# One order of the vector work for all inner images, weight taps copied by two engines, and the group mean of x added while x1 is copied

## What is computed

```python
# stage 1, for 8 images b, 64 channels c, on the map padded by one pixel (26 x 26)
g       = group_norm(x)
off     = conv3x3(pad(g), w_off)              # 2 offsets (dy, dx) per channel and pixel
sampled = bilinear(pad(g), grid + off)        # inner 24 x 24 pixels
x1      = x + einsum(relu(batch_norm(sampled) * gamma + beta), w_pw)
# stage 2
cov = covariance(group_norm(x1))              # 64 x 64 for each image
v   = mean_rows(newton_schulz_sqrt(cov, 5 iterations))
a   = sigmoid(w2 @ relu(w1 @ v + b1) + b2)
out = x1 + a * group_norm(x1)
```

## Time and profile before

| | |
|---|---|
| median of 3 runs | 100.12 us (99.66 to 100.27) |
| profiled execution, its own time | 100.33 us |
| its span (first to last instruction) | 98.1 us |
| PE busy / share of the span | 83.1 us (85%) |
| DVE busy | 77.7 us (79%) |
| ACT busy | 63.9 us (65%) |
| chain that ended last, by engine | PE 41%, DVE 35%, ACT 9%, issue 6%, DMA 4% |

### The profile page before, as it was taken

One profiled execution on the slowest core, in us unless ns is written; L12 is line 12 of the kernel. 1 busy time (PEld: TensorE's weight loads), 2 busy tenths in 40 slices (PEclk: granted clock), 3 DMA queues, 4 the chain that ended last, 5 costly groups with the idle time before them and its releaser, 6 DMA issues.

```text
span 98.1 us, 2359 instructions
## 1 busy us (share of the span) xinstructions
PE 83.1 (85%) x873; PEld 58.4 (60%) x873; DVE 77.7 (79%) x262; ACT 63.9 (65%) x141; POOL 17.3 (18%) x41
## 2 busy tenths in 40 slices
PE   5995999999999999999980399999899999898200
PEld 4873655455545554555650289999788888786200
DVE  6659859998699999999999999889945548764420
ACT  2328369995999899877889789249222237784440
POOL 7964997000000000000000482000000000000000
PEclk9999999999999999999998557999999999999555
DMA  2584741989969695693030005000000000000066
GB/s 39 201 260 145 171 136 36 199 262 233 231 176 198 184 189 179 145 246 120 0 120 3 0 0 170 0 0 0 0 7 0 0 3 7 0 0 7 0 246 235
DMA packets 5483, 10.18 MB, mean 104 GB/s; under 512 B 1216, under 2 KB 2272, under 8 KB 5472
## 3 DMA queue, kind: packets, MB, share of 16 engines
q1 hardware_dynamic: 4784, 9.29, 34.6%
q0 software_dynamic: 528, 0.45, 1.8%
q10 hardware_dynamic: 160, 0.30, 1.0%
HBM read 1.92 MB, written 5.14 MB: 72 GB/s over the span
## 4 chain that ended last, share of the span: by engine, by line
PE 41%; DVE 35%; ACT 9%; issue 6%; DMA 4%; ACTq 1%; DVEq 0%
PE ps L702 15%; PE ps L736 7%; DVE rows_at_x L976 6%; PE ps L839 5%; PE ps L780 4%; DMA x_pairs<-in_x_dram 4%; ACT relu_out L610 3%; DVE rows_at_x L991 3%; PE ps L746 3%; DVE rows_at_x L985 3%; DVE row_difference L971 3%; DVE rows_at_x L997 2%; DVE largest_abs_offset L965 2%; DVE neighbour_row L987 2%; DVE rows_at_x L1000 2%
## 5 line engine op out<-in xcount | busy, mean ns | idle before, releaser
L702 PE MATMUL ps<-gmap,w_off_taps 128*64 128x288 f32 (+1 forms) x384 | 38.3, 414 | 1.1 <-DVE w_off_taps L945 1.1
L702 PEld LDWEIGHTS ps<-gmap,w_off_taps 128*64 128x64 f32 (+1 forms) x384 | 19.7, 133 | 18.8 <-issue 6.1
L495 ACT COPY rows_at_x<-x_differences 128x864 f32<-128x864 f32 x8 | 7.3, 916 | 3.2 <-DVE x_differences L953 2.1
L442 POOL DMA_INDIRECT slot_offset<-offset_scratch,gather_rows x1 | 2.1, 2068 | 38.4 <-DVE gather_rows L1056 38.4
L976 DVE COPY_PREDICATED rows_at_x<-positive_offsets,x_differences 128x864 f32<-128x864 int32 x7 | 8.3, 1184 | 0.4 <-ACT positive_offsets L506 0.4
L506 ACT ACTIVATE positive_offsets<-ps 128x576 f32<-128x576 f32 x8 | 5.2, 650 | 4.0 <-PE ps L702 4.0
L488 ACT ACTIVATE gmap<-x_pairs,gn_shift,gn_rstd 64x576 f32<-64x576 f32 x8 | 7.0, 879 | 0.5 <-DVE gn_shift L935 0.4
L736 PEld LDWEIGHTS ps<-ident,x_pairs 128*96 128x96 f32 x48 | 6.7, 198 | 0.4 <-issue 0.4
L736 PE MATMUL ps<-ident,x_pairs 128*96 128x128 f32 x48 | 6.9, 316 | 0.0
L520 ACT ACTIVATE abs_offsets<-offsets 128x576 f32<-128x576 f32 x8 | 6.6, 826 | 0.2
L746 PE MATMUL ps<-w_pw_blocks,relu_out 128*96 128x128 f32 x48 | 6.3, 281 | 0.0
(11 more groups left out here) (209 smaller groups left out, 169.2 us busy)
## 6 DMA issues: line engine op xcount, KB each, us to landing
offset_scratch<-offsets SPq DMA_DIRECT2D x8, 288.0 KB, 3.3
hmap<-gmap SPq DMA_DIRECT2D x16, 98.0 KB, 2.5
gmap_scratch<-gmap SPq DMA_DIRECT2D x8, 196.0 KB, 3.2
gmap<-gmap SPq DMA_DIRECT2D x7, 189.0 KB, 2.8
x_pairs<-in_x_dram SPq DMA_DIRECT2D x4, 288.0 KB, 3.4
out_dram<-result SPq DMA_DIRECT2D x4, 288.0 KB, 2.6
w_off_natural<-in_L_conv_w_off_dram ACTq DMA_DIRECT2D x2, 144.0 KB, 3.8
w_natural<-in_L_conv_w_dram POOLq DMA_DIRECT2D x4, 2.0 KB, 2.4
```

What stands on the lines that cost most here:

```text
L495: nc.scalar.copy(rows3(hrow[:, par]), windows(dx[:, par, 0:HH, 0:W], 3, MC - 1)).then_inc(left_ok, 1)
L702: return mm(ps[out, 2 * par + chunk, 0:Q], wt[rows, slot, out], conv_window(gmap[rows, b], at, NP), start=start, stop=stop)
```

## The change

The images 1 to 6 (`EARLY`) all get image 1's order on DVE: `second_image` becomes `early_image(b, par)` with general indices, and `image_step` is left with images 0, 7 and the closing step. On ACT `left_differences(b)` moves ahead of `positive_parts(b)` for these images. The copy of the first three weight taps is split: ACT copies two (256 columns) ahead of `fill_gmap(0)`, DVE the third (128 columns). `copy_natural` becomes an activation with the mean as its bias, so `x1` holds the mean; the shift becomes `c1 = attention * (rstd * (offset - mean))`, with the factor in parentheses computed by two new small DVE instructions ahead of the pooled vector, and the last four small DVE instructions become three.

```diff
+    EARLY = range(1, 7)
...
             gn1_std(1, 0, 1)
+            act.wait_ge(wtrans, 1)
+            nc.scalar.copy(wt[:, 0:2, :].rearrange("p a n -> p (a n)"), ps[:, 5, 0:2 * P]).then_inc(pairs_ok, 1)
             act.wait_ge(gn1_ok, 1)
...
-                if b == 1:
-                    left_differences(1, 1)
+                if b in EARLY:
+                    left_differences(b, b % 2)
                 positive_parts(b, b % 2)
...
-                    if b > 1:
+                    if b not in EARLY:
                         left_differences(b, b % 2)
                     far_mask(b - 1)
...
-                nc.scalar.copy(x1[:, j], ps[:, NAT_BANK[j % 3], 0:Q]).then_inc(nat_ok, 1)
+                nc.scalar.activation(x1[:, j], ps[:, NAT_BANK[j % 3], 0:Q], ACT.Identity,
+                                     bias=mv1[:, j // 2, 0:1]).then_inc(nat_ok, 1)
...
-                    pe.wait_ge(pairs_ok, 1)
+                    pe.wait_ge(pairs_ok, 2)
...
             dve.wait_ge(wtrans, 1)
-            v.tensor_copy(wt[:, 0:3, :].rearrange("p a n -> p (a n)"), ps[:, 5, 0:3 * P]).then_inc(pairs_ok, 1)
+            dve.wait_ge(pairs_ok, 1)
+            v.tensor_copy(wt[:, 2, :], ps[:, 5, 2 * P:3 * P]).then_inc(pairs_ok, 1)
...
-            def second_image():
+            def early_image(b, par):
+
+                h, g = hrow[:, par], hrow[:, 1 - par]
+                dve.wait_ge(along, 4 * b)
                 v.tensor_tensor(vd[:], g[:, 0], g[:, 1], ALU.subtract).then_inc(across, 1)
+                dve.wait_ge(across, 2 * b - 1)
+                v.tensor_tensor(vd[:], vd[:], ab[:, 1 - par, 0], ALU.mult).then_inc(across, 1)
+                dve.wait_ge(across, 2 * b)
+                v.tensor_tensor(xd[:, b - 1], vd[:], g[:, 1], ALU.add).then_inc(image_done, 1)
+                dve.wait_ge(left_ok, b + 1)
+                dve.wait_ge(pos_ok, b + 1)
...
+                differences(b + 1, 1 - par)
...
-            second_image()
-            for b in range(2, B - 1):
-                image_step(b, b % 2)
+            for b in range(1, B - 1):
+                if b in EARLY:
+                    early_image(b, b % 2)
+                else:
+                    image_step(b, b % 2)
             image_step(B - 1, 1, ahead=False, between=locate_slot)
...
+            v.tensor_tensor(rstd_offset[:], vals[:, 1], mv1[:, :, 0], ALU.subtract).then_inc(rstd_offset_ok, 1)
+            dve.wait_ge(rstd_offset_ok, 1)
+            v.tensor_tensor(rstd_offset[:], rstd_offset[:], vals[:, 0], ALU.mult).then_inc(rstd_offset_ok, 1)
             dve.wait_ge(vec_ps, 1)
...
             dve.wait_ge(att_ok, 1)
-            link(v.tensor_tensor(ar[:], att[:], vals[:, 0], ALU.mult))
-            then(v.tensor_tensor(c1[:], ar[:], vals[:, 1], ALU.mult))
-            v.tensor_scalar(s1[:], ar[:], 1.0, None, ALU.add)
+            dve.wait_ge(rstd_offset_ok, 2)
+            then(v.tensor_tensor(ar[:], att[:], vals[:, 0], ALU.mult))
+            then(v.tensor_tensor(c1[:], att[:], rstd_offset[:], ALU.mult))
             wait()
-            v.tensor_tensor(c1[:], c1[:], mv1[:, :, 0], ALU.add).then_inc(out_scale_ok, 1)
+            v.tensor_scalar(s1[:], ar[:], 1.0, None, ALU.add).then_inc(out_scale_ok, 1)
             dve.wait_ge(out_scale_ok, 1)
```

More of the change, by code:

```diff
@@ L109, in deform_conv_then_covariance_attention @@
         count = sb("far_count", [P, 1])
+        rstd_offset = sb("rstd_times_offset", [P, T])
         most = sb("far_images_and_places_beyond_two", [1, 1])
@@ L290, in deform_conv_then_covariance_attention @@
         att_ps = sem("attention_in_psum")
+        rstd_offset_ok = sem("rstd_times_offset_ready")
         out_scale_ok = sem("out_scale_ready")
@@ new lines, in early_image @@
+                dve.wait_ge(across, 2 * b - 1)
[4 more added lines that the diff above has]
+                dve.wait_ge(pos_ok, b + 1)
+                v.copy_predicated(rows3(h), windows(rows(pos[:, par, 1, :]), 3, 0).bitcast(i32),
+                                  windows(dx[:, par, 0:HH, 1:1 + W], 3, MC - 1)).then_inc(along, 1)
@@ new lines, in early_image @@
+                differences(b + 1, 1 - par)
+                dve.wait_ge(along, 4 * b + 1)
+                v.copy_predicated(h[:, 0], pos[:, par, 0, :].bitcast(i32), h[:, 2]).then_inc(chosen, 1)
+                dve.wait_ge(above_ok, b + 1)
+                v.copy_predicated(rows(mrow[:, par]), rows(pos[:, par, 0, :]).bitcast(i32),
+                                  hmap[:, b, 2:2 + HH, 1:1 + W]).then_inc(chosen, 1)
+                dve.wait_ge(chosen, 2 * b + 1)
+                dve.wait_ge(off_ok, b + 1)
@@ L1030, in second_image @@
+                v.tensor_tensor(h[:, 0:2], h[:, 0:2], windows(off[:, b, :, 1], 2, 0), ALU.mult).then_inc(along, 1)
+                dve.wait_ge(abs_ok, b + 1)
+                v.tensor_tensor(far[:, b], ab[:, par, 0], ab[:, par, 1], ALU.max).then_inc(far_ok, 1)
+                dve.wait_ge(along, 4 * b + 2)
+                v.tensor_tensor(rows(h[:, 1]), rows(h[:, 1]), hmap[:, b, 1:1 + HH, 1:1 + W],
                                 ALU.add).then_inc(along, 1)
-                dve.wait_ge(chosen, 4)
@@ L1032, in second_image @@
-                v.tensor_tensor(h[:, 0], h[:, 0], mrow[:, 1], ALU.add).then_inc(along, 1)
+                dve.wait_ge(chosen, 2 * b + 2)
+                v.tensor_tensor(h[:, 0], h[:, 0], mrow[:, par], ALU.add).then_inc(along, 1)
             def zero_far(g, b0, b1):
```

23 lines of the change are left out of this document (removed).

## The result

| | before | changed |
|---|---|---|
| median of 20 runs each, same chips | 100.25 us (99.30 to 101.38) | 100.69 us (100.02 to 101.62) |
| ratio of the times, 95% interval | | 1.0062 [1.0032, 1.0092] |
| profiled execution, its own time | 100.33 us | 101.32 us |
| its span | 98.1 us | 99.1 us |
| mean granted TensorE clock, share of full | 0.927 | 0.945 |

The change makes the kernel 0.6% slower, within the 1% called "no change" ahead of it. The forecast was 100.6 us. A ratio leaves out executions over 1.5% above the fastest of their kernel: one of the 20 of the changed kernel, and further down three of 12 of the kernel with only image 7's list new, four of 12 where that kernel has no pairs. Executions of one kernel also differ by their mean granted clock.

A forecast was written before the change was run, and what follows sets the result against it. DVE's own throughput from 25.3 to 54.3 us was taken to set the end. +0.52 (image 7, start included) + 0.09 (bias) - 0.12 (end) = +0.49 on 100.12 gave 100.6 us; own range 100.2 to 101.1, 8 in 10 99.7 to 101.5.

The forecast's parts named there:

- What bounds it: DVE's own throughput from 25.3 to 54.3 us sets the end; counts and transposes hang on the release by `gather_rows`.
- The wait goes, three stalls come: DVE, images 2 to 6: the 1.12 us wait goes; three stalls of 0.12 make an image 5.47 instead of 5.12.
- The first rival, no stalls: Dependent pairs on DVE cost nothing, images stay 5.12 us: -0.82 with the edges, 99.3 us; chance 0.12.
- the larger stall: Rival: each dependent pair on DVE costs 0.19 us, an image takes 5.69; 101.8 us; chance 0.13.
- The wait at image 7: Image 6's mask on ACT waits for `far(6)` and delays image 7's copies; DVE's copy at 51.72 instead of 51.20, +0.52 us.
- ACT's slack: ACT's idle time of 0.45 us ahead of the counts shrinks to 0.18, so the release moves by 0.52.
- The start: Split tap copy: PE's first convolution 0.27 us earlier, ACT's copy hidden in 0.42 of idle time ahead of its first map.
- The mean and the end: Bias in the last copy of x1 costs +0.09 us; fewer closing DVE instructions give -0.12.
- The two copies between Newton-Schulz rounds: ACT's copies with the bias there might cost up to 0.09 us each; counted only in the range.
- The clock: Rival: PE's clock returns to the high level 1 us later against the work, costing 0.5: 101.1 us; chance 0.12.
- +0.79 for the order: Order change on DVE and ACT without the start's gain: image 7's 864-element copy comes 0.79 us later.
- -0.03 for the rest: Closing part: -0.12 us for one link less, +0.09 for the longer last copy ahead of the hidden layer.

The follow-up runs named there:

- the kernel with only image 7's list new: Changed kernel with ACT's two copies for image 7 (`left_differences(7)`) ahead of the mask of image 6; 100.4 us, ratio to before 0.9998.
- where that kernel has no pairs: Spread DVE order without dependent pairs, with only `left_differences(7)` moved ahead of the mask of image 6 on ACT; ratio to before 0.9935.
- the two fastest kernels: Spread DVE order, ACT's signs ahead of `left_differences` for images 3 to 6, `left_differences(7)` ahead of mask 6; with the change's end 0.9868, without it 0.9848.
- three experiments: Order change alone on the kernel before (1.005); changed kernel with `left_differences(7)` moved (0.9998); that plus signs first for images 3 to 6 on ACT (1.0048).
- The kernel without pairs: Changed kernel, but images 2 to 6 keep DVE's interleaved order, with `far` moved from second to third from last; 99.43 us, ratio to before 0.9927.
- the start alone: The kernel before with only the tap copy split between ACT and DVE; 100.5 us, ratio 1.0002.
- the kernel without pairs with the new list: Spread DVE order, ACT's signs ahead of `left_differences` for images 3 to 6, `left_differences(7)` ahead of the mask of image 6; 98.9 us, ratio to before 0.9868.
- pairs and the new list: Changed kernel, DVE order kept, ACT's signs ahead of `left_differences` for images 3 to 6, `left_differences(7)` ahead of the mask of image 6; ratio to before 1.0048.
- the order alone: The kernel before with only the change's order on DVE and ACT, neither start nor end; 100.73 us, ratio 1.005.

## Why the prediction was right, point by point

- **What bounds it: right.** `gather_rows` stands 3.02 to 3.11 us behind DVE's copy of image 7 in every kernel, and the counts follow it, except in the two fastest kernels, where ACT's own list is the later of the two.
- **The wait goes, three stalls come: right, and it decides the sign.** The stall of 0.12 was read off one image and holds in each: 0.49 or 0.50 against 0.37. The forecast had 5.47 us an image; 5.48 to 5.50 in three experiments, 5.52 in the changed kernel. The kernel without pairs takes 1.3% off. The first rival, no stalls, falls with this, and so does the larger stall: the late duration of 0.53 didn't return in the changed kernel, where these instructions last 0.44 to 0.48. The Trainium skill, VectorE: DVE Perf Modes, The DRAIN you can't avoid, says that the next instruction waits for an empty pipe, so that a semaphore between neighbours costs nothing extra; it adds only that "A next op that is not held starts earlier", and gives no price for a dependence. On that price the traces disagree: independent neighbours start 0.37 apart, less than the duration of 0.46, and the dependence costs that overlap. Whether the data or the semaphore wait that guards them takes the 0.12, no run separates; with another instruction between the two, the same wait costs nothing.
- **The wait at image 7: the mechanism right, its place right in part by luck.** Forecast: mask to next start 0.65, `far(7)` to copy 0.98. Measured: 0.53 (51.29 to 51.82) and 0.85. The 0.65 was the distance from a mask to the small `image_excess_signs`; a copy follows a mask sooner. Against that the five images took 0.19 more (24.48 to 51.90, where the forecast has 23.51 to 50.74). Moved by the start's own 0.98 (15.17 where the forecast has 14.19), the forecast's 51.72 for the copy becomes 52.70; it was 52.75. The shorter way from mask to copy and the longer images cancel there.
- **ACT's slack: about right.** 0.18 was to be left ahead of the counts; 0.12 was, and nothing was lost.
- **The start: wrong in the profiled execution, right elsewhere.** The step said that ACT's copy lies in 0.42 of idle time. That rests on PE having the taps ready. Where PE took 1.75 us, the convolution came 0.26 earlier relative to `gn_shift`; where it took 2.84, the copy was in the way of `fill_gmap(0)` and the gain was nought. The timing of the start alone shows no gain, and its interval doesn't exclude the 0.26. The step named the price of a lost cover but looked for its loss on ACT, not at what ACT's copy waits for.
- **The mean and the end: sizes off.** -0.12 was measured as -0.11, and the last copy as +0.11 where 0.09 was taken. These two still made -0.03 from the last copy of x1 to the output, as `hidden` is followed a little sooner. The two copies between Newton-Schulz rounds, put only into the range, cost 0.08 together. So the -0.03 of these terms should have been +0.05.
- **The clock: no loss.** TensorE fell to the low level (1.2 of 2.4 GHz) in the pause ahead of the counts, as before. Windows of the changed kernel (us; busy share of PE, its loads, DVE, ACT, POOL; granted clock; DMA), answering:

```profile
54.00:55.00 1.00, 0.00 (x0) 0.00 (x0) 1.00 (x7) 0.97 (x5) 0.00 (x0) 0.53 0.00 0
...
60.00:61.00 1.00, 1.00 (x8) 1.00 (x7) 0.93 (x3) 1.00 (x3) 0.79 (x3) 0.56 0.52 69
61.00:62.00 1.00, 1.00 (x12) 1.00 (x11) 0.93 (x3) 0.97 (x5) 0.00 (x0) 1.00 0.73 100
```

The clock rose at about 60.9, before at about 59.9 (estimates from the means of 0.56 and 0.54 in those windows), 1.0 later, while the work had moved by 1.50, so fewer transposes ran slowly, and 0.26 came back between `gather_rows` and the batch-norm product. This differs from execution to execution: from the product of the counts on PE to the batch-norm product it took 8.13 before, 7.87 here, 8.93 in the kernel without pairs with the new list, whose gain is partly eaten by it. The clock's second fall, at the end, came later than before and gave 0.21 in this execution, as said under **The end**; the prediction didn't look there.

**The sum.** The forecast's +0.49 is +0.79 for the order, -0.27 for the start and -0.03 for the rest. Measured: order +0.66 at the copy of image 7 and +0.5 in the time, start between -0.26 and nought, end about +0.05. That gives +0.3 to +0.7, and the timing says +0.6 with an interval of +0.3 to +0.9. So the mechanism that decides the sign held, and the closeness of +0.49 is in part luck: the order was put 0.13 too high, the end 0.08 too low, and a start that gains nothing in part of the executions is on top of that.

What stays open: how often an execution has the slow start. It is in the profile of the changed kernel and in that of the kernel with image 7's list; nine of the twenty runs of the changed kernel lie at 101.2 to 101.6, one of them the profiled execution, and nothing ties the other eight to it. Nor is it shown whether the split copy makes such executions more frequent: at 101.17 or above lie these nine of 20, three of 12 with image 7's list alone, four of 12 with pairs and the new list, but one of 12 with the order alone, which has no split copy. The 0.5 between medians at a mean clock from 0.947 up is free of all nine.

## What to carry to other kernels

Before moving an instruction to end one wait, count the instructions that will then read what the one directly ahead wrote: on DVE each cost 0.12 us here, on tiles of 128x288, and the loop over images paid it in every round, while the wait was paid once. Cure a wait where it is (one image, or by moving the one instruction that waits) and keep the interleaving elsewhere. When work goes onto an engine's idle time, ask what the moved instruction waits for, not only whether the engine is free.

## What the runs showed of the hardware

- A DVE instruction on 128x288 that reads its predecessor's result starts 0.49 us behind it, an independent one 0.37; its own duration is shown as 0.46 in both cases. So the independent ones overlap by 0.09 us, and the dependent one starts 0.03 behind the end of the other. With one other instruction between the two, the dependence costs nothing (L997 reads what L991 wrote, with `sampled` between them, and starts 0.37 behind `sampled`).
- PE's 24 first transposes took 1.74 to 1.92 us in eleven traces and 2.84 or 2.85 in two, with a granted clock of 1.00 recorded in both kinds (in the window from 6 to 7 us, 11 records in the changed kernel and 20 before); the first convolution records were slower there too (6 in 1.38 us, before 6 in 0.95). What made PE slow there, the rows don't show.
- PE's two small products for the attention took 0.38 us with a granted clock of 1.00 and 0.59 with 0.50.
- A pointer bias adds 0.10 us to ACT's copy of 288 elements out of PSUM (0.50 against 0.40).
